# Cross-attention with a routed FFN: the subtraction for P's lower half, placed right behind the row maxima on VectorE

## What is computed

```
q = split_heads(layernorm(x) @ Wq.T);  k, v = split_heads(ctx @ Wk.T), split_heads(ctx @ Wv.T)
scores = einsum('bhqd,bhkd->bhqk', q, k) * D_MODEL ** (-0.5) + attn_bias
weights = softmax(scores, axis=-1)
x = x + merge_heads(einsum('bhqk,bhkd->bhqd', weights, v)) @ Wp.T
x = x + expert_ffn(layernorm(x))
```

## Time and profile before

| | us |
|---|---|
| median of 3 runs (lowest to highest) | 1057.69 (1055.72 to 1057.95) |
| the profiled execution | 1060.19 |
| its span | 1058.4 |
| busy in the span: PE / DVE / ACT / POOL | 984.5 / 889.0 / 840.1 / 727.7 |

### The profile page before, as it was taken

One profiled execution on the slowest core, in us unless ns is written; L12 is line 12 of the kernel. 1 busy time (PEld: TensorE's weight loads), 2 busy tenths in 40 slices (PEclk: granted clock), 3 DMA queues, 4 the chain that ended last, 5 costly groups with the idle time before them and its releaser, 6 DMA issues. The chain is left out here.

```text
span 1058.4 us, 47454 instructions
## 1 busy us (share of the span) xinstructions
PE 984.5 (93%) x13640; PEld 808.5 (76%) x13640; DVE 889.0 (84%) x3981; ACT 840.1 (79%) x2536; POOL 727.7 (69%) x1086
## 2 busy tenths in 40 slices
PE   4899999999999999999999999983799999999995
PEld 3788888888888888888888888972366666766664
DVE  4998999999999999999999999975766665656553
ACT  5888999999999999999999999951666567566562
POOL 6576777777777777777777777761277677677673
PEclk9999999999999999999999999975899999999998
DMA  3998888989888888988898889880011111111212
GB/s 107 161 165 148 168 174 162 173 168 174 162 173 168 173 166 169 171 171 168 166 172 170 167 168 173 171 151 6 1 31 30 34 58 30 50 50 31 61 40 70
DMA packets 440585, 130.91 MB, mean 124 GB/s; under 512 B 417504, under 2 KB 433888, under 8 KB 440544
## 3 DMA queue, kind: packets, MB, share of 16 engines
q1 hardware_dynamic: 439680, 128.24, 62.6%
q10 hardware_dynamic: 864, 2.16, 0.6%
HBM read 16.58 MB, written 4.19 MB: 20 GB/s over the span
## 5 line engine op out<-in xcount | busy, mean ns | idle before, releaser
L443 ACT ACTIVATE probs<-neg,negmax 128x120 f32<-128x120 f32 x1024 | 320.2, 387 | 51.0 <-DVE negmax L472 50.3
L472 DVE CUSTOM_DVE_ANT_0 neg<-bk_s,bias_sb 128x120 f32<-128x120 f32 x1024 | 225.0, 273 | 4.4 <-PE bk_s L604 3.8
L299 POOL CAST parts<-probs 128x480 f16<-128x480 f32 x256 | 155.4, 607 | 96.3 <-ACT probs L443 96.3
L1147 POOL TENSOR_TENSOR hid<-hid_f,hid 128x512 f16<-128x512 f32 x128 | 167.6, 1313 | 74.9 <-ACT hid L1101 73.9
L307 POOL TENSOR_TENSOR parts<-o_sb,parts 128x256 f16<-128x256 f32 x256 | 171.8, 671 | 47.3 <-ACT parts L408 46.8
L604 PE MATMUL bk_s<-qk 64*128 64x120 f32 x2048 | 182.4, 297 | 1.9 <-DVE negmax L472 1.4
L556 DVE TENSOR_TENSOR parts<-probs,parts 128x480 f16<-128x480 f32 x256 | 171.2, 669 | 0.0
L1201 DVE TENSOR_TENSOR hid_f<-bk_u,silu 128x512 f32<-128x512 f32 x128 | 88.4, 690 | 86.2 <-ACT silu L1094 35.0
L604 PEld LDWEIGHTS bk_s<-qk 64*128 64x128 f32 x2048 | 135.3, 187 | 23.0 <-issue 2.2
L400 ACT COPY qk<-bk_a 128x496 f32<-128x496 f32 x256 | 146.3, 572 | 3.6 <-PE bk_a L591 3.4
L647 PE MATMUL bk_o<-v_hi,w_f 120*128 120x65 f16 x1024 | 121.6, 196 | 1.5 <-DMA w_f<-parts 1.5
(11 more groups left out here) (165 smaller groups left out, 3520.5 us busy)
## 6 DMA issues: line engine op xcount, KB each, us to landing
y_all<-y SPq DMA_DIRECT2D x128, 64.0 KB, 2.0
wst<-ffn_w SPq DMA_DIRECT2D x64, 96.0 KB, 2.5
w_f<-parts SPq DMA_TRANSPOSE x260, 3.7
x_sb<-x SPq DMA_DIRECT2D x64, 64.0 KB, 2.3
out<-x_sb SPq DMA_DIRECT2D x16, 256.0 KB, 2.0
ctx_f<-ctx_t SPq DMA_DIRECT2D x64, 60.0 KB, 2.4
w_f<-wqkv_t ACTq DMA_DIRECT2D x3, 512.0 KB, 5.5
wp_sb<-wp_t ACTq DMA_DIRECT2D x1, 512.0 KB, 6.3
```

What stands on the lines that cost most here:

```text
L299: pool.tensor_copy(p_parts[g][:, 0, :, 0:K], probs[g % 2][:, :, :]).then_inc(p_hi_ready, 1)
L443: e = nc.scalar.activation(probs[g % 2][:, i, :], neg[g % 2][:, i, :], ACT.Exp, bias=negmax[g % 2][:, i:i + 1], scale=-1.0)
L472: r = nc.vector.tensor_tensor_reduce(out=neg[g % 2][:, i, :], in0=bk_s[i % 2][:, (i // 2) * K:(i // 2 + 1) * K], in1=bias_sb[:, :], scale= ...
L1147: nc.gpsimd.tensor_tensor(hid[1][par][:, ic, :], hid_f[ic % 2][:, :], hid[0][par][:, ic, :], ALU.subtract).then_inc(hid_lo_ready, 1)
```

## The change

The subtraction for P's lower half (its wait on `p_hi_ready`, the instruction and its signal) stands right behind the row maxima of each step and no longer at the step's end. It still handles the group of the step before. Nothing else is changed; the programs of the other engines are the same instruction by instruction.

```diff
                             accum_out=negmax[g % 2][:, i:i + 1])
                     r.then_inc(neg_ready, 1)
+                b1, g1 = behind(t, g, 1)
+                if live(b1):
+
+                    dve.wait_ge(p_hi_ready, 4 * b1 + g1 + 1)
+                    nc.vector.tensor_tensor(p_parts[g1][:, 1, :, 0:K], probs[g1 % 2][:, :, :],
+                                            p_parts[g1][:, 0, :, 0:K], ALU.subtract).then_inc(p_lo_ready, 1)
                 if g == 0:
                     if live(t + 1):
                         dve.wait_ge(x_stats_ready, t + 2)
...
-                b1, g1 = behind(t, g, 1)
-                if live(b1):
-
-                    dve.wait_ge(p_hi_ready, 4 * b1 + g1 + 1)
-                    nc.vector.tensor_tensor(p_parts[g1][:, 1, :, 0:K], probs[g1 % 2][:, :, :],
-                                            p_parts[g1][:, 0, :, 0:K], ALU.subtract).then_inc(p_lo_ready, 1)
                 if isinstance(t, int) and t == 1 and g == 0:
```

## The result

The changed kernel takes **1149.78 us** (median of 6 runs, 1149.23 to 1150.46) beside 1057.76 for the kernel before on the same chip: a ratio of 1.0875, 95% interval 1.0862 to 1.0887. It is 92 us slower; 73 were forecast, inside a range up to 1160. The profiled execution has a span of 1147.4.

The account below looks back on a forecast made before the run. VectorE's order and holds were taken to bound the attention part; 10.48 + 0.76 + 0.24 + 0.40 = 11.88 us per slot, 1.28 over the mean, x 57 = 73 us on 1057.7: 1131 us, range 1078 to 1160.

Parts of the forecast that it names:

- Step 1, +0.76: In step 1 the early subtraction waits 0.67 for POOL's cast and instructions behind it are held; step 2's maxima start 0.76 us later.
- case A: In step 1 the subtraction goes before POOL's `lower_o`, which ends after it; slot 11.88 us, 1131 us; the case taken.
- case B: In step 1 POOL's `lower_o` goes first and the subtraction ends at 1.80; slot 12.04 us, 82 us slower, 1140 us.
- Step 2, +0.24: In step 2 the subtraction is held and ends 0.52 after `lower_o`; its successor starts 0.24 us later.
- step 3, +0.40: In step 3 the subtraction is held again by `lower_o`; its successor starts at 7.40, not 7.00, 0.40 us more.
- Step 0, 0: In step 0 the subtraction meets only the tail of `lower_o`, at no cost.
- The slot: VectorE's stretch of four steps, one subtraction each: forecast 11.88 us, against a mean of 10.60 and an undisturbed 10.48.
- No hold (1079): Rival: subtraction and `lower_o` don't hold each other; slot 10.97 us, 21 us slower, 1079 us; chance 0.18.
- Faster (1051): Rival: transposes start earlier and TensorE's waits for them go; slot 10.48 us, 7 us less, 1051 us; chance 0.05.
- Nothing to measure: Rival: the new waits only replace holds of equal size, time unchanged within about 0.2% (2.1 us); chance 0.04.
- Signs: Expected in the profile: idle 0.6 us per slot before step 1's subtraction, `rstd` about 0.7, longer subtractions or `lower_o`, `xn` at least 0.6.
- H: Follow-up theory: the loss is `lower_o` holding the subtraction in steps 1 to 3 plus step 1's new wait for the cast.

Follow-up runs that it names:

- step 0 alone: Against the kernel before, the subtraction moved right behind the row maxima in step 0 only, left at the step's end in the others: 1080.90 us, ratio 1.0216.

## Why the prediction was right, point by point

**VectorE sets the stage.** Right. All that the subtraction lost in durations and waits appeared in the slot, and the added slack of TensorE, ScalarE and the transposes covered what I had costed at nothing: TensorE waits 48.6 us for `v_lo`, and VectorE never waits for its scores.

**Step 1, +0.76: the mis-sized term.** I took case A, the subtraction ahead of `lower_o`. In each of the 41 slots looked at `lower_o` had started 0.07 before it and went first, which was case B, sized at +0.92. Measured, from the end of step 1's maxima to the start of step 2's, 0.58 of idle and 0.08 for the last maximum and 3.39 - 0.81 to the next maxima's start (3.39 from the subtraction's start to that of step 2's) make 3.24, and 3.27 in the other half of the slots, against 2.26 before: **+0.99**. The wait was 0.58 and 0.70, forecast 0.67. My row for A was `rstd`, which stood although it had started 0.02 ahead. It didn't carry over to `lower_o`; why the two differ stays open. The Trainium skill's rule (SBUF — State Buffer, Who interferes with whom), by which whoever issues first takes the shared ports for its whole instruction, gave case B and 1140 us; here the trace agrees with it (0.07 ahead, 0.51 to 0.52 after), while `rstd` in the kernel before still doesn't.

**Step 2, +0.24, and step 3, +0.40.** Right: 0.86 and 1.06 in place of 0.64, which is 0.22 and 0.42.

**Step 0, 0.** Right in the changed kernel (0.65), but not in general: moved alone, step 0 costs 23 us.

**The slot.** 10.48 + 0.99 + 0.22 + 0.42 = 12.11 against a forecast of 11.88 and 12.04 for case B. The mean of 12.21 lies 0.10 higher because slots of 12.08 and 12.36 alternate (from step 2's maxima to the next), as 10.47 and 10.75 did before. The longer ones have it in step 3, where a gap of about 0.12 stands behind each of the two `bn_stats`. I had put the 0.12 between 10.60 and 10.48 down to TensorE being late behind transposes, and let it vanish with them. They vanished and the alternation didn't, and the kernel before doesn't bear the reading out: VectorE waits for TensorE for 0.4 us in its 400,

```profile
DVE rsum L509 <- PE bk_o L649: 0.4, 2, 0.2
```

where 38 slots times 0.12 would be 4.6. What causes the alternation stays open.

**The rivals.** No hold (1079) falls with the durations beside `lower_o`; 1084.24 for the kernel without `lower_o` is about the time that it gave. Faster (1051) fails at its condition: the cast came 0.58 to 0.70 too late. The condition met and the holds gone, in the kernel without `lower_o` and with the cast ahead, 1053.79 is close to its figure. Nothing to measure falls too.

**Signs.** As named: idle before step 1's subtraction, `rstd` at 0.69, the mean at 0.922, `lower_o` at 0.67, no wait for the transposes, the clock at 1.00. Not as named: `xn` at 0.43 and not 0.6 or more, because in case B it meets the last part of `ctx_lo` and not `lower_o`.

## What to carry to other kernels

Where VectorE and POOL both work on SBUF, place an instruction not only by when its input is there but by what POOL runs at that moment: such a meeting shows in no list of waits, only as a longer duration of one of the two. Lay the two timelines side by side before moving a step, and follow the queue of both engines for a whole slot, since each hold shifts what the next step meets; of the twelve times above five fell outside the range that H gave, and the two widest misses (step 0 alone, and `lower_o` behind the subtraction) came from stopping one step too early. And a chain between two engines, here `vpe`, `rstd`, cast, subtraction, should keep other work between its links on the engine that both starts and ends it.

## What was not expected of the hardware

How late a held subtraction ends did not depend on how early it came: started 0.07, 0.12 or 0.32 us after `lower_o`, the subtraction ended 0.50 to 0.53 after it. And taking POOL's work away can make VectorE slower: with `lower_o` reduced to one element the kernel before rose from 1057.43 to 1061.62, because another POOL instruction, `xn_lo`, came ahead of a VectorE one.
